# Attention outputs and norms tile by tile in one block, weights ahead, and the last two stages of a graph network in one block

## What is computed

```python
# layer 0, gnn: attention masked by the graph's edges, h = norm(x); x = x + attention(h, mask) @ Wo + bo
# layer 0, ffn: h = norm(x); a = h + attention(h) @ Wo + bo
#               n = (a - mean) * rsqrt(var + 1e-5) * ln1_g + ln1_b
#               logits = n @ gate_W + gate_b; the one best of 8 experts with its softmax weight
#               x = x + weight * (gelu(n @ W1[e] + b1[e]) @ W2[e] + b2[e])
# layer 3, gnn ("sage"): h = norm(x); A = neighbours' mean of h; for each of 4 experts e:
#               h1 = relu(h @ Wr[e,0] + A @ Wl[e,0] + b0[e])
#               o = mean over neighbours(h1 @ Wl[e,1]) + h1 @ Wr[e,1] + b1[e]
#               x = x + gate_weight[e] * relu(o)
# layer 3, ffn: n = norm(x); logits = n @ router_w; the two best of 8 experts, softmax over the two
#               x = x + sum_k weight_k * ((silu(n @ Wg[e]) * (n @ Wu[e])) @ Wd[e])
```

## Time and profile before

| | |
|---|---|
| runs, median (lowest to highest) | 2002.68 us (1997.71 to 2006.96) |
| the profiled execution's own time | 1999.71 us |
| its span, first to last instruction | 1998.0 us |
| TensorE busy, products | 1868.6 us, 94% |
| TensorE busy, loads of the fixed operand | 1029.5 us, 52% |
| VectorE, ScalarE, GpSimd busy | 48%, 25%, 16% |
| moved by DMA | 358.00 MB, 179 GB/s on average |
| mean granted TensorE clock | 0.978 of full |

### The profile page before, as it was taken

How to read it: one execution, slowest core, us unless ns; L and a number is a source line. 1 busy time by engine, 2 the same in 40 slices (tenths; PEclk the granted TensorE clock), 3 DMA queues, 4 the chain that set the end, 5 groups by cost and what they waited for, 6 DMA issues and landing times. The chain is left out here.

```text
span 1998.0 us, 27190 instructions
## 1 busy us (share of the span) xinstructions
PE 1868.6 (94%) x8875; PEld 1029.5 (52%) x8875; DVE 959.9 (48%) x2901; ACT 501.7 (25%) x1381; POOL 321.1 (16%) x345
## 2 busy tenths in 40 slices
PE   8999979999899999999999799889789999989999
PEld 4464548667544434533553333334334444468876
DVE  9662653000269877997799611156433223331102
ACT  1270631111134351244225312146110000010000
POOL 0000001334337304720670000000000000010001
PEclk9999999999999999999999899989899999989999
DMA  5003039997277306720677389952361220099884
GB/s 168 0 2 105 1 127 371 398 353 290 59 263 219 111 1 220 204 70 12 197 206 264 114 316 387 348 166 89 131 213 47 90 90 0 4 351 389 316 324 154
DMA packets 180665, 358.00 MB, mean 179 GB/s; under 512 B 28816, under 2 KB 38304, under 8 KB 180524
## 3 DMA queue, kind: packets, MB, share of 16 engines
q1 hardware_dynamic: 157548, 285.94, 39.8%
q0 software_dynamic: 22976, 70.23, 11.8%
HBM read 334.43 MB, written 21.69 MB: 178 GB/s over the span
## 5 line engine op out<-in xcount | busy, mean ns | idle before, releaser
L1147 PEld LDWEIGHTS ps<-tokT,w 128*128 128x128 f32 x2304 | 259.8, 192 | 10.7 <-issue 6.7
L1147 PE MATMUL ps<-tokT,w 128*128 128x128 f32 x2304 | 260.6, 275 | 3.1 <-DVE tokT L1292 3.1
L1606 POOL DMA_INDIRECT w<-xl_d,src_i x216 | 214.6, 994 | 290.7 <-DMA xl_d<-XL 222.6
L1702 PE MATMUL ps<-XP,wide 128*128 (+1 forms) x456 | 185.3, 507 | 0.0
L1707 PE MATMUL ps<-w,ident 128*128 128x512 f32 x270 | 140.9, 603 | 8.0 <-DMA w<-xl_d,src_i 7.4
L1702 PEld LDWEIGHTS ps<-XP,wide 128*128 128x128 f32 x456 | 81.5, 188 | 72.6 <-issue 67.4
L1817 ACT ACTIVATE wide<-oht 128x128 fp32r<-128x128 bf16 x228 | 68.1, 308 | 198.7 <-PE ps L1707 178.8
L1166 PE MATMUL ps<-w,O 128*128 128x512 f32 x256 | 111.2, 592 | 0.0
L1306 DVE TENSOR_TENSOR hT<-act,ps 128x512 f32<-128x512 f32 x20 | 13.8, 688 | 181.4 <-ACT act L1199 181.4
L1979 DVE SCALAR_TENSOR_TENSOR w<-ps,w 128x512 f32<-128x512 f32 x144 | 98.1, 682 | 5.1 <-PE ps L1707 4.8
L878 POOL MEMSET gate<- 128x96 f32 (+1 forms) x3 | 0.5, 183 | 587.7 <-POOLq L667 277.4
(11 more groups left out here) (532 smaller groups left out, 3031.1 us busy)
## 6 DMA issues: line engine op xcount, KB each, us to landing
w<-L_ffn_W SPq DMA_DIRECT2D x16, 2048.0 KB, 13.6
w<-L_ffn_W SPq DMA_DIRECT2D x8, 4096.0 KB, 19.4
w<-fc1T SPq DMA_DIRECT2D x32, 1024.0 KB, 14.2
w<-fc2T SPq DMA_DIRECT2D x30, 1024.0 KB, 14.2
w<-L_ffn_w_gate SPq DMA_DIRECT2D x20, 1024.0 KB, 9.7
w<-L_ffn_w_up SPq DMA_DIRECT2D x20, 1024.0 KB, 12.2
w<-L_ffn_w_down SPq DMA_DIRECT2D x10, 2048.0 KB, 15.8
w<-L_ffn_w SPq DMA_DIRECT2D x8, 2048.0 KB, 13.7
```

Source lines behind the costliest of these rows:

```text
L1147: m = pe.matmul(k.ps[:, 1 + (q * ins + i) % 4, s * P:(s + 1) * P], self.W1[u][i][:, f, (q * T + s) * P:(q * T + s + 1) * P], self.tokT[:, ...
L1606: gp.indirect_dma_start(self.G[:, u, :], None, k.xl_d, bass.IndirectOffsetOnAxis(ap=k.src_i[:, i:i + 1].bitcast(U32), axis=0)).then_inc(k. ...
L1702: m = pe.matmul(bank, self.wide[:, i % DEEP, :], self.XP[:, q].rearrange("p t n -> p (t n)")[:, bass.ds(at, D)], start=False, stop=(q == 1 ...
```

## The change

Five edits, made together:

1. **Weights ahead.** The four weight tiles `W` and two sets of bias vectors are made outside the attentions. The second attention's loads are issued in the first attention's block, each as soon as the products with the old weights of that buffer are done. The block of `layernorm` is gone.
2. **Outputs and norm by tile.** The last two head pairs' output products run for tiles 0 and 1, then tile 2, then tile 3. A new class `TileNorm` does the norm of one tile at a time behind VectorE's add, in the same block.
3. **Scale and shift in copies.** `ln1_g` and `ln1_b` are no longer applied to `k.N`. They are laid out one per partition and applied by ScalarE as it copies turned tiles to `NT`, and by VectorE as it copies `tokT` (four pieces of 128 columns instead of one copy).
4. **Gate by rows.** In the second attention and in the last sage expert the gate is a product with the turned tile as the fixed operand (`row_logits`), 16 products of 8 columns, and no strips to add up. The gate's loads and the clears of `spread` move into the second attention's block.
5. **Sage and last FFN in one block.** The loop is written out; L3000 and L3007 alternate by tile in all experts; in the last one norm, transposes and gate products go by tile; the FFN's clears and first weights are issued in sage, whose weight buffers are now those of the FFN.

`counts.means` moves ahead of Q's bias copies. The core of the diff:

```diff
+def attention_weights(sp, k, w, W, vectors):
+    for dst, src in zip(vectors, (w["bq"], w["bk"], bcast(w["bv"]), bcast(w["bo"]))):
+        sp.dma_start(dst[:], src).then_inc(k.loaded.sem, 16)
+    for j, m in enumerate((w["Wq"], w["Wk"], w["Wv"], w["Wo"])):
+        sp.dma_start(W[j][:], rows_of(m)).then_inc(k.slot[j].sem, 16)
...
+            def _(sp):
+                if more is not None:
+                    more(sp)
+                if following is not None:
+                    w_next, vectors_next = following
+                    for dst, src in zip(vectors_next, (w_next["bq"], w_next["bk"], bcast(w_next["bv"]),
+                                                       bcast(w_next["bo"]))):
+                        sp.dma_start(dst[:], src).then_inc(k.loaded.sem, 16)
+                    for j, m in enumerate((w_next["Wq"], w_next["Wk"], w_next["Wv"], w_next["Wo"])):
+                        sp.wait_ge(k.mm.sem, k.mm.at(T * (j + 1)))
+                        sp.dma_start(W[j][:], rows_of(m)).then_inc(k.slot[j].sem, 16)
+
...
-                    for t in range(T):
+                    for t in tiles:
                         m = pe.matmul(k.ps[:, t, :], OT[:, f, t * P:(t + 1) * P], W[3][:, f, :],
                                       start=(f == 0), stop=(f == T - 1))
                         if f == T - 1:
...
-                    if n >= STEPS:
+                    if STEPS <= n < STEPS + 2:
                         result(n - STEPS)
-                result(T - 1)
+                result(2, (0, 1))
+                result(3, (0, 1))
+                for t in (2, 3):
+                    result(2, (t,))
+                    result(3, (t,))
+                for t in range(T):
+                    if t == T - 1:
+                        keep_busy(pe, k, 2, 8)
+                    closing.turn(pe, t, T + t)
+                if gate is not None:
+                    for t in range(T):
+                        closing.wait_columns(pe, t)
+                        gate.row_logits(pe, t, 0)
 
             @block.vector
...
                     counts.degrees(v, ch)
+                    counts.means(v, ch)
...
-                    v.tensor_tensor(out[:, t, :], out[:, t, :], k.ps[:, t, :], ALU.add)
+                    ch.link(v.tensor_tensor(out[:, t, :], out[:, t, :], k.ps[:, t, :], ALU.add))
+                    closing.statistics(v, ch, t)
+                    if t:
+                        closing.normal(v, ch, t - 1)
+                closing.normal(v, ch, T - 1)
...
+                for t in range(T):
+                    closing.roots(a, t)
+                    if t:
+                        closing.columns(a, t - 1, T + t - 1)
+                closing.columns(a, T - 1, 2 * T - 1)
...
+    def row_logits(self, pe, t, bank):
+
+        k, width = self.k, self.width
+        if t == 0:
+            pe.wait_ge(self.gate_loaded.sem, self.gate_loaded.at(32 if self.bias is not None else 16))
+        for f in range(T):
+            m = pe.matmul(k.ps[:, bank, t * 8:t * 8 + width], self.cols[:, f, t * P:(t + 1) * P],
+                          self.g[:, f, 0:width], start=(f == 0), stop=(f == T - 1))
+        if t == T - 1:
+            m.then_inc(self.gate_turned.sem, 1)
+
...
+    def statistics(self, v, ch, t):
+        ch.link(v.bn_stats(self.st[:, t, :], self.x[:, t, :]))
+        v.bn_aggr(self.mv[:, t, :], self.st[:, t, :]).then_inc(self.stats.sem, 1)
+
+    def roots(self, a, t):
+        a.wait_ge(self.stats.sem, self.stats.at(t + 1))
+        a.activation(self.rstd[:, t:t + 1], self.mv[:, t, 1:2], ACT.Sqrt, bias=self.k.eps[:, 0:1]
+                     ).then_inc(self.root.sem, 1)
+
+    def normal(self, v, ch, t):
+        v.wait_ge(self.root.sem, self.root.at(t + 1))
+        ch.link(v.reciprocal(self.rstd[:, t:t + 1], self.rstd[:, t:t + 1]))
+        v.tensor_scalar(self.rows[:, t, :], self.x[:, t, :], self.mv[:, t, 0:1], self.rstd[:, t:t + 1],
+                        ALU.subtract, ALU.mult).then_inc(self.normed.sem, 1)
+
+    def turn(self, pe, t, bank):
+        pe.wait_ge(self.normed.sem, self.normed.at(t + 1))
+        for f in range(T):
+            m = pe.transpose(self.k.ps[:, bank, f * P:(f + 1) * P], self.rows[:, t, f * P:(f + 1) * P],
+                             self.k.ident[:])
+        m.then_inc(self.turned.sem, 1)
+
+    def columns(self, a, t, bank):
+        a.wait_ge(self.turned.sem, self.turned.at(t + 1))
+        if self.gain_cols is not None:
+            if t == 0:
+                a.wait_ge(self.k.gain_loaded.sem, self.k.gain_loaded.at(32))
+            for f in range(T):
+                m = a.activation(self.cols[:, f, t * P:(t + 1) * P], self.k.ps[:, bank, f * P:(f + 1) * P], ACT.Identity,
+                                 bias=self.gain_cols[:, 1, f:f + 1], scale=self.gain_cols[:, 0, f:f + 1])
+            m.then_inc(self.cols_out.sem, 1)
+            return
+        a.activation(self.cols[:, :, t * P:(t + 1) * P],
+                     self.k.ps[:, bank, :].rearrange("p (f n) -> p f n", f=T), ACT.Copy).then_inc(self.cols_out.sem, 1)
...
+            if self.gain_cols is None:
+                m = v.tensor_copy(self.tokT[:].rearrange("p k n -> p (k n)"), k.ps[:, 0, :])
+            else:
+                for f in range(T):
+                    m = v.tensor_scalar(self.tokT[:, f, :], k.ps[:, 0, f * P:(f + 1) * P], self.gain_cols[:, 0, f:f + 1],
+                                        self.gain_cols[:, 1, f:f + 1], ALU.mult, ALU.add)
+            m.then_inc(k.ffn_cols.sem, 1)
...
+                ffn.r.sync(sp)
+                ffn.empty(sp)
+                ffn.second_weights(sp, 0, 0)
+                sp.wait_ge(k.heads.sem, k.heads.at(E - 1))
+                ffn.first_weights(sp, 0, 0)
+                ffn.sync(sp)
...
+                        if e == E - 1 and t >= 2:
+                            closing.wait_columns(pe, t - 2)
+                            ffn.r.row_logits(pe, t - 2, 0)
+                        if t == 0:
+                            pe.wait_ge(k.ready.sem, k.ready.at(1 + e))
                         for part in (hi, lo):
                             for s in range(T):
                                 m = pe.matmul(k.ps[:, T + t, :], k.C[:, s, t * P:(t + 1) * P], part[:, s, :],
                                               start=(part is hi and s == 0), stop=(part is lo and s == T - 1))
                         m.then_inc(k.out.sem, 1)
-                walk(pe, step)
+                        if e == E - 1 and t:
+                            closing.turn(pe, t - 1, t - 1)
+                for e in range(E):
+                    step(e)
+                closing.wait_columns(pe, T - 2)
+                ffn.r.row_logits(pe, T - 2, 0)
+                keep_busy(pe, k, 5, 12)
+                closing.turn(pe, T - 1, T - 1)
+                closing.wait_columns(pe, T - 1)
+                ffn.r.row_logits(pe, T - 1, 0)
+                ffn.tensor(pe)
 
             @block.scalar
...
+                        if e == E - 1:
+                            ch.link(m)
+                            closing.statistics(v, ch, t)
+                            closing.normal(v, ch, t)
```

More of the change, by code:

```diff
@@ L731, in weigh, with result @@
                                 i.then_inc(k.av.sem, 1)
-                def result(f):
+                def result(f, tiles=range(T)):
                     pe.wait_ge(k.heads.sem, k.heads.at(f + 1))
@@ L797, in _ @@
                                     ).then_inc(k.copied.sem, 1)
-                if counts is not None:
-                    counts.means(v, ch)
                 minima(0)
@@ L848, in attention @@
             counts.done()
+        if gate is None:
+            closing.done()
 class Routing:
@@ L956, in done, with __init__ @@
     def done(self):
-        k = self.k
-        done((k.gate_loaded, 32 if self.bias is not None else 16), (k.gate_padded, 1), (k.gate_mm, 1), (k.gate_rows, 1), (k.gate_turned, 1), (k.gate_ready, 1), (k.gate_exped, 1))
+        done((self.stats, T), (self.root, T), (self.normed, T), (self.turned, T), (self.cols_out, T))
 class RoutedFfn:
-    def __init__(self, k, c, r, norm, granules, w, hidden, gated, spread, result, beside=None, spare=None, y=None):
+    def __init__(self, k, c, r, norm, granules, w, hidden, gated, spread, result, beside=None, spare=None, y=None,
+                 joined=False):
@@ L1282, in vector @@
         k, quads = self.k, self.quads
-        self.norm.vector(v)
+        if not self.joined:
+            self.norm.vector(v)
         self.r.vector(v, chosen=self.choose)
@@ L1408, in run @@
     def run(self):
[L1409 to L1410 removed]
+        with self.k.nc.Block() as block:
             @block.sync
@@ L2921, in sage @@
         with nc.Block() as block:
-            def walk(eng, step):
-                for u in range(2):
-                    step(u, u, 0)
-                with eng.Fori(1, E // 2) as j:
-                    for u in range(2):
-                        step(j * 2 + u, u, j)
```

(5 more changed lines are left out.)

239 lines of the change are left out of this document (136 added, 103 removed).

## The result

The changed kernel ran in 1989.01 us (median of 6 runs, 1985.63 to 1995.61), the kernel before in 2002.99 (6 runs, 1997.71 to 2006.96): a ratio of 0.9935, 95% interval 0.9914 to 0.9956. Two further sets of runs gave 0.9931 [0.9917, 0.9946] and 0.9953 [0.9938, 0.9967]. The profiled execution took 1985.63 us, its span is 1983.8 instead of 1998.0, its mean granted clock 0.984 instead of 0.978.

The account below looks back on a forecast made before the run. TensorE is busy 94% of the span, so only three junctions where it idles or runs slowly can pay: 1.8 + 3.2 + 7.2 = 12.2 us off 1999.7 gives 1987.5, plus 3.0 for the median, 1990.5; range 1983.5 to 1999.

Parts of the forecast that it names:

- First junction, 1.8: Between the two attentions: Q starts 8.1 us after T, the last output product's end, instead of 9.9; gain 1.8 us.
- Weights ahead gain nothing by themselves: First junction: issuing weights early gains nothing alone, because Wq had already landed as the barrier opened.
- `means` at nothing: Second attention: moving `means` ahead of Q's bias copies is worth nothing; its 16.4 us fall where VectorE idles.
- The 1.2 us that I left to the low clock: Q's 32 products after the first junction: 1.2 us lost to the low clock, kept as a loss in the forecast.
- Second junction, 3.2: Second attention to its routed FFN: gain 3.2 us, with a 2.4 us wait appearing on the second token tile's DMA.
- compute alone gives 5.6: Second junction: earlier FFN start gains 6.7 us, less table load and piecewise scaling, leaving 5.6 before counting the weights' DMA.
- Third junction, 7.2: Sage to the last FFN: logits at T+7.0 instead of 14.6, 2.7 us paid earlier, token wait of 2.34 gone; gain 7.2.
- a sign of being wrong: Sage: the forecast would be wrong if sage's experts took longer than before; no size given.
- The clock rival, 0.17: All junctions: TensorE's short bursts keep its clock at the lower level, taking 8 us off the gain, 1998.5; chance 0.17.
- DMA did bind: Second junction: rival that DMA does not bind the FFN's start, or the clock stays full, 1986 us; chance 0.13.
- Links were not longer than summed: All junctions: rival that tile-by-tile links take longer than summed, each junction 1.5 us less, 1995; chance 0.10.
- the slower side: Sage: rival that 12 more switches between product kinds cost 0.41 us each, 4.9 in all, 1995; chance 0.05.

Follow-up runs that it names:

- e2: Kernel before with only sage and the last FFN in one block as changed, both attentions and their norms as before: ratio to before 0.9957.
- e4: Changed kernel with the second attention's four weight matrices issued only at the first attention's last output product: Q starts 7.69 us after that product.
- e1: Changed kernel with both attention junctions kept, but sage, its norm and the last FFN as before: ratio to before 0.9988.
- e5: The changed kernel run again, unaltered, to see its spread: ratio to before 0.9931.
- e7: Changed kernel without attention fillers, second attention's gate products placed between the turns: that junction's logits 11.32 us after the last output product, against 11.94.
- e6: Changed kernel with the first FFN's first W1 and b1 loaded during the second attention into a free buffer: 1993.7 us.
- e11: The changed kernel run a third time, unaltered, on the chip of a version with further edits: ratio to before 0.9953.
- e3: Changed kernel without the filler products in the attentions and sage: last junction, to the second expert's products, 39.19 us against 37.47.
- e9: Changed kernel with W1 loaded ahead and no fillers in attentions or sage: last junction, to the second expert's products, 40.16 us against 37.47.
- e10: Changed kernel with W1 ahead, gate products between turns, VectorE turn copy and early exponential table, alternating sage's products only in the last expert: ratio to before 0.9929.
- e8: Changed kernel with W1 ahead, gate products between turns without attention fillers, VectorE copying the last turn and the exponential table loaded early: ratio to before 0.9915.

## Why the prediction was right, step by step

The forecast was 1990.5 (gain 12.2), the result 1989.0. The total is right; one term is not, and the clock made up for it. So the mechanism held in the first and the third junction, and that the sum still came out is in part luck: the second junction fell short by 3.5 us, and the profiled pair differs by 4.8 us in places where I had put nothing (1.0 ahead of the first T, 1.5 in the Q and K products, 2.3 behind sage's T, of clock).

- **First junction, 1.8.** At full clock on both sides, from the first T to the second: 116.88 in e2 and 114.98 in the changed kernel, 1.9. Steps: VectorE's pace per tile came as summed (the adds of the last three tiles start 2.14 and 2.18 us apart), the last tile was ready at T+4.5 for T+4.8, the fillers held its turn, and Q started at T+7.7 for T+8.1. "Weights ahead gain nothing by themselves" is shown by e4. `means` at nothing holds: V's products began at 82.77 and at 82.13, within the 0.64 by which the whole start moved. (A product is 7.13/8 = 0.89 us; the 0.86 in the prices is the distance from one to the next.) The 1.2 us that I left to the low clock were not lost in this profile; they are lost or not from run to run.
- **Second junction, 3.2: this step failed.** To the second token turn the profiled pair shows -0.3 (41.81 and 42.09), and the turn came at T+42.1 where the sum has T+38.6. Of these 3.5 us, 1.4 are the block's start, T+11.9 instead of T+10.5. The filler ahead of the last turn ran at a granted clock of 0.67 (280.1 to 282.5) and ended the turn at T+8.1 instead of T+7.2; the gate products, at full clock, took 3.64 us instead of 2.95, as a pass costs 0.11 us and not the 0.09 that I took from products of 128x16. The other 2.0 lie behind the block's start: W2 and b2 were there 29.4 us later where I had summed 27.4, and the tile 0.7 behind them, as written. That the wait came to 2.59, for 2.4, is luck: the first products were late as well, at T+24.6, not at T+21.4. From logits to first products it was 12.66, where I had 9.82 + 1.05; the placing products and the fillers ran at a low clock, and in e1, e5 and e7, where the placing products did not, it was 11.0. So "compute alone gives 5.6" gave 2.5.

  The order in the queue is what held: the tile comes behind W2 and b2, and e6 removed that cause and the wait with it. It also means that work on the chain to the logits pays here by no more than the weights are issued earlier. In all seven profiles that issue them at the block's start the turn comes 29.9 to 30.2 us behind the logits, however early the first products are. By the Trainium skill ("DMA: Bandwidth & Descriptors", Queues, rings and completion order) a row's transfers are consumed in order; e6 agrees.

  The size of the gain is less certain than one pair makes it. From the first T to the second token turn two profiles of the old code (before, e2) have 160.5 and 161.4, four of the new (after, e1, e5, e11) 156.9 to 160.0, a mean gain of 2.9; to the end of that FFN the mean gain is 1.9, as two of the four waited 4.2 us and went on at the lower clock. e1's ten runs have 2.4 (0.4 to 4.4). The sum had 5.0 for both junctions, and nothing for the clock behind the wait.
- **Third junction, 7.2.** Logits at T+7.0, as summed. Ahead of T sage pays 3.3 (224.8 less 221.5): 2.8 in the last expert, forecast 2.7, and 0.5 in the first three, for which I had nothing and which I had named as a sign of being wrong. The 2.34 us of waiting are gone: the token tile landed 2.5 us after its issue and the writes 2.7 to 3.8. From sage's T to the second expert's products the gain is 12.8 gross; less 3.3 it is 9.5, where 7.2 was summed. The rest is clock: before, the first expert's 16 second products took 8.52 behind the wait (the clock was at 0.50 from 1786 to 1788), now 7.03, and logits to first products went from 9.67 to 8.76. e2 by itself gives 8.6 (6.2 to 10.8).
- **The clock rival, 0.17,** had a true mechanism and failed in its direction: it wanted a lower clock than before in each junction, and the first and the last were at 1.00, the second at 0.86 for 0.81. In the last, twelve fillers stand in the longest pause; without them (e3, e9) the clock falls and it costs 1.7 and 2.7 us. In the first, the dip comes or stays away in either code. The Trainium skill ("TensorE: Matmul & The Clock Gate", HAM oscillation) says that waits for DMA between bursts of products let the clock fall, so that the next burst starts at the lower level; the token turns behind waits of 3.6 to 4.2 us (e1, e3, e4, e5, e7) and the one behind 2.34 us before sage was changed agree, those behind 2.4 and 2.6 us (e11, after) do not show it.
- **The other rivals.** DMA did bind. Links were not longer than summed (the last junction is exact). A switch between L3126 and L3136 costs nothing that e10 can find, and e10 takes away nine of the twelve, so the slower side had no mechanism.

## What to carry to other kernels

A chain turned from stage-wise to tile-wise pays by its own links where nothing else ends at the same place; before counting it, find which transfer is next in line, and whether that transfer's issue moves with the chain. Here the clears moved out of the way, the weights behind them did not move up, and the compute gain in that junction was returned as a wait; moving the first weights into the stage before removed it. A wait can cost more than its length: look at the clock of what follows it. Filler ahead of a critical instruction has a price, its length, which doubles when the clock is low already (1.7 and 3.6 us here), and against it stand the dips it prevents. Try both, in each place by itself, and compare stretches between the same events in several profiles.

## What was not expected of the hardware

Apart from the clock the timing repeats to 0.02 us: 37.46 or 37.47 us in the last junction in nine profiles, 79.66 to 79.68 from the first scores to T in the attention in all thirteen. What spreads the times of these kernels is where the granted clock falls: Q and K took 27.63, 29.2 to 29.4, or 30.6 us for the same products, and the untouched middle of the kernel 1421.6 to 1435.8 us. The same code on TensorE met the dip in the first junction in one profile of six (e1, against after, e4, e5, e6, e11). The wait for one token tile was between 2.4 and 4.2 us in the same code, and decided whether the 32 products behind it took 13.90 us or 15.85. Within a junction, gate products of 128x8 took 0.11 us a pass in the changed kernel and 0.21 in e7 and e8.
